# A graph kernel's first layer: TensorE takes the gathered tiles ahead of the count matmuls in each half turn

## The reference, cut to what matters

```python
proj = einsum('nf,hfg->nhg', x, w_proj)
delta = proj[sender] - proj[receiver]
radial_logits = einsum('ehf,hf->eh', delta, radial_score) - scale * edge_len[:, None]
tangential_logits = einsum('ehf,hf->eh', delta, tangential_score)
# per receiver: alpha = softmax of the logits over its edges; sum of alpha * delta
out = seg_softmax_msg(radial_logits) + seg_softmax_msg(tangential_logits)
x = layernorm(x + (x + nan_to_num(out.mean(axis=1)) @ w_out))
```

## Time and profile before

| | |
|---|---|
| median of 3 runs | 3445.18 us (3444.8 to 3448.61) |
| the profiled execution | 3443.76 us, its span 3442.0 us |
| mean granted TensorE clock | 0.725 of full speed |
| busy over the span | PE 2513.1 us, DVE 2112.7, POOL 1797.3, ACT 433.8 |
| the changed stage's first and last gather | start at 134.6 and 1278.3 us |

### The profile page before, as it was taken

The page is one execution under the profiler, slowest core; times in us unless marked ns, Lnnn a source line. Parts: engine busy times, 40 slices in busy tenths (PEclk is TensorE's granted clock), DMA queues, the critical chain, the costliest instruction groups (busy, mean ns, idle before and its releaser), DMA issues. The chain is left out here.

```text
span 3442.0 us, 63721 instructions
## 1 busy us (share of the span) xinstructions
PE 2513.1 (73%) x13080; PEld 1967.7 (57%) x13081; DVE 2112.7 (61%) x7932; ACT 433.8 (13%) x1043; POOL 1797.3 (52%) x1867
## 2 busy tenths in 40 slices
PE   1477777777777776896647634888888899888836
PEld 1244454444444443554637633888888888888826
DVE  5477777777777764543332332777777777777743
ACT  0011111111111111111000001111111111111100
POOL 0377777777777760000010011777777777777710
PEclk6699989999999997997857855555555555555558
DMA  1344444444444451000000001333333333333410
GB/s 36 95 119 120 122 119 119 122 122 117 121 122 119 120 111 26 16 12 1 7 0 1 1 1 34 80 82 81 81 81 82 81 82 82 82 81 82 79 18 10
DMA packets 415827, 246.81 MB, mean 72 GB/s; under 512 B 327579, under 2 KB 372618, under 8 KB 415754
## 3 DMA queue, kind: packets, MB, share of 16 engines
q0 software_dynamic: 71040, 176.52, 20.2%
q1 hardware_dynamic: 281786, 47.96, 7.4%
q10 hardware_dynamic: 62928, 21.43, 2.4%
HBM read 231.37 MB, written 14.34 MB: 71 GB/s over the span
## 5 line engine op out<-in xcount | busy, mean ns | idle before, releaser
L860 POOL DMA_INDIRECT edges_rows<-table,edges_idx x888 | 874.4, 985 | 273.0 <-issue 213.9
L1672 POOL DMA_INDIRECT edges_rows<-table_kv,edges_idx x888 | 855.6, 964 | 276.7 <-issue 257.6
L983 PE MATMUL edges_radial_ps<-edges_rows,edges_into_w 128*128 x1776 | 480.4, 408 | 237.4 <-SPq L870 212.9
L983 PEld LDWEIGHTS edges_radial_ps<-edges_rows,edges_into_w 128*128 128x128 f32 x1776 | 322.2, 194 | 390.1 <-issue 352.2
L1863 PE MATMUL edges_acc<-edges_values,edges_into 128*128 128x136 f32 x1776 | 511.4, 461 | 41.8 <-DVE edges_values L1752 31.3
L1863 PEld LDWEIGHTS edges_acc<-edges_values,edges_into 128*128 128x128 f32 x1776 | 416.6, 328 | 81.0 <-DVE edges_values L1752 66.3
L915 DVE TENSOR_SCALAR edges_cell<-edges_ramp,edges_strip_key,first_key 128x400 bf16<-128x400 f16 x1184 | 452.7, 382 | 0.0
L1840 PE MATMUL edges_q_ps<-attention_q,edges_into_t 128*128 (+1 forms) x1782 | 441.8, 421 | 0.0
L1840 PEld LDWEIGHTS edges_q_ps<-attention_q,edges_into_t 128*128 128x128 f32 x1782 | 416.3, 334 | 0.0
L1717 DVE TENSOR_SCALAR edges_ahead<-edges_nodes,edges_starts,edges_dst_f 128x128 bf16<-128x128 f32 x894 | 261.2, 358 | 174.7 <-issue 174.7
L914 DVE TENSOR_SCALAR edges_low<-edges_places,first_src_low 128x128 bf16<-128x128 bf16 x1184 | 329.2, 278 | 0.1
(11 more groups left out here) (343 smaller groups left out, 2241.4 us busy)
## 6 DMA issues: line engine op xcount, KB each, us to landing
edges_values<-in_edge_attr SPq DMA_DIRECT2D x888, 32.0 KB
edges_rows<-table,edges_idx POOLq DMA_INDIRECT x888
edges_rows<-table_kv,edges_idx POOLq DMA_INDIRECT x888
edges_attr<-in_edge_attr ACTq DMA_DIRECT2D x51, 256.0 KB
edges_bias<-bias_kept SPq DMA_DIRECT2D x296, 12.0 KB
bias_kept<-edges_bias_out ACTq DMA_DIRECT2D x52, 64.0 KB
table<-all_counts SPq DMA_DIRECT2D x1, 3250.0 KB, 11.4
radial<-edges_radial_out ACTq DMA_DIRECT2D x25, 130.0 KB
```

Source lines behind the costliest of these rows:

```text
L860: pool.indirect_dma_start(rows[:, n, :], None, table0, bass.IndirectOffsetOnAxis(ap=idx[:, n:n + 1], axis=0)).then_inc(s_rows[g], 16)
L983: last = nc.tensor.matmul(radial_ps[:, 0:ROW0], into_w[:, h, j, :], rows[:, bass.ds(slot + h * G + j, 1), :].squeeze(1), start=False, stop ...
L1672: pool.indirect_dma_start(rows[:, n, :], None, table_kv, bass.IndirectOffsetOnAxis(ap=idx[:, n:n + 1], axis=0)).then_inc(s_rows[g], 16)
```

## The change

In each half turn PE now waits for the landed rows and for `into_w` first and does the three matmuls of gathered rows; then it waits for the one-hots of the counts and does the four count matmuls, and the last of these raises `s_half`. No instruction is added or removed, and the loops of the other engines stand as they were.

```diff
                                     for h in range(2):
-                                        pe.wait_ge(s_fro, 2 * v + h + 1)
-                                        for q in range(Q):
-                                            nc.tensor.matmul(cells_ps[:, q, 0:KEY], low[:, h, q, :], cell[:, h, q, :], start=False, stop=True,
-                                                             skip_group_check=True)
                                         pe.wait_ge(s_landed, 2 * v + h + 5)
                                         pe.wait_ge(s_into, 2 * v + h + 2)
                                         for j in range(G):
-                                            last = nc.tensor.matmul(radial_ps[:, 0:ROW0], into_w[:, h, j, :],
-                                                                    rows[:, bass.ds(slot + h * G + j, 1), :].squeeze(1),
-                                                                    start=False, stop=True, skip_group_check=True)
+                                            nc.tensor.matmul(radial_ps[:, 0:ROW0], into_w[:, h, j, :],
+                                                             rows[:, bass.ds(slot + h * G + j, 1), :].squeeze(1),
+                                                             start=False, stop=True, skip_group_check=True)
+                                        pe.wait_ge(s_fro, 2 * v + h + 1)
+                                        for q in range(Q):
+                                            last = nc.tensor.matmul(cells_ps[:, q, 0:KEY], low[:, h, q, :], cell[:, h, q, :], start=False, stop=True,
+                                                                    skip_group_check=True)
                                         last.then_inc(s_half, 1)
```

## The result

The changed kernel ran at 3517.94 us (median of 4, 3517.39 to 3518.94) against 3446.0 us for the kernel before in the same comparison: a ratio of 1.0208, 95% interval 1.019 to 1.0226. The forecast was 3448 us, its range ended at 3462 us. It was wrong.

The account below looks back on a forecast made before the run. The prediction took POOL's gathers to bound the stage. It summed 0 (steady) + 2 (low clock) + 0.7 (end) + 0 (gathers) to about +3 us on 3443.76, giving 3446.8, and 3448 us as median; range 3435 to 3462 us.

Parts of the forecast that it names:

- What bounds the kernel: Changed stage: POOL's gathers bound it at 23.3 us a side; DVE at 22.25 us has 1.0 us to spare.
- PE's work and the start of the tiles: PE in each half: tiles start unchanged, priced at nothing; `s_half` comes 2.26 us after it instead of 1.58.
- the low clock: Short low-clock stretches of the stage: counts before `s_half` take 1.1 us more per half; priced at 2 us, at most 12.
- the clock rival: Side starts: PE stands still some 1 us longer, clock falls more often; five sides at 4.7 us, 3470 us; chance 0.13.
- the delay doesn't pile up from side to side: DVE's index copies: fourth half's tiles hang on the rows' landing, so POOL resets DVE each side; steady sides cost nothing.
- The cover: Next side's index copy ahead of its gather: 2.7 us, 2.1 us at a window's start, against a copy 0.46 us late.
- DVE's loop as the bound at full clock: Rival: PE's tile-to-count switch costs 0.15 us more, so DVE's side reaches 23.3 us; 3450 to 3460 us; chance 0.10.
- POOL's wait for row buffers: POOL waits for the half four before, ended over two halves of 3.88 us earlier; 0.68 us delay covered: nothing.
- the end of the stage: After the last tiles, count matmuls now precede ACT's cast: +0.68 us, once; other side ends 0.
- The gathers: POOL's gathers slowed beside DVE: 34 us of excess dealt anew, bounds 17 us less or more, middle nothing.
- What would have shown it: Wrong if POOL pauses before line 860 exceed 5 us in sum, clock under 0.9, or mean gather over 8 ns from 985.
- signs of being right: POOL's gathers back to back in about 1144 us, DVE's short waits for PE well over a hundred, PE's landed-row wait grown.

Follow-up runs that it names:

- e12: Kernel before with one more DVE instruction in each half, a comparison into a spare tile that nobody reads: 3479.2 us, profiled execution 3469.27 us.
- e7: Changed kernel with one of the three `into_w` of each half left out on DVE, so the radial sums are not the reference's: 3435.47 us.
- e1: Changed kernel with 18 added matmuls of zeros on PE at each side's start, behind the clears: 3444.96 us.
- e10: Kernel before with 5 matmuls of zeros between tiles and `s_half`, plus 18 at each side's start: eleven runs from 3439.68 to 3445.43 us.
- e9: Kernel before with 18 matmuls of zeros on PE at each side's start: ratio 0.9994.
- e2: Kernel before, counts still first, with 5 matmuls of zeros between the gathered tiles and `s_half`: ten runs from 3436.11 to 3492.17 us.
- e6: Changed kernel with 9 added matmuls of zeros on PE at each side's start: ten runs from 3446.65 to 3481.10 us.
- e5: Kernel before with one added wait: in each turn's first half PE waits for `into_w` before the counts, which still stand first: 3478.35 us.
- e8: Changed kernel's PE order, with DVE making the three `into_w` before the eight one-hots of the counts: 3451.99 us.
- e11: Kernel before with tiles first only in each turn's second half, plus 18 matmuls of zeros at each side's start: 3450.84 us.
- e4: Kernel before with tiles first only in each turn's second half: nine of ten runs at 3438.9 to 3447.1 us, one at 3456.2.

## Why the prediction was wrong

**What bounds the kernel: right.** POOL bound the stage before, DVE was second, and e12 and e7 show both sides of its margin. The margin was read a little too large: 22.25 us is the side without line 893, and every second side has some 0.65 us more on DVE, so that the mean slack against 23.3 us is an estimated 0.7 us and not 1.0.

**PE's work and the start of the tiles: half right.** Tiles and counts together take 2.25 us at full clock (645.34 to 647.59 in the changed kernel's timeline), forecast 2.26. But "the start is unchanged" held only where rows came last, and in the changed kernel they did so four times (4.8 us of waits for them).

**The step that failed is the low clock.** The forecast took the clock of before as given, 50 us of low stretches, looked at what the new order costs inside them, and priced that at 2 us in its sum, at most 12. Measured, POOL's new pauses are 95.0 us, of which shorter gathers gave 22.9 back. The change made new low stretches: in the changed kernel there is one at 48 of 50 side starts, and the clock over the stage is 0.90 for 0.98. The clock was not a setting under which the change runs, it was one of its results. The delay of one `s_half` was well worked out in the clock rival: 3.7 to 4.2 us behind the tiles, measured 3.95 and 4.30. The rival counted five sides at 4.7 us; it was nearly all 50, at 1.4 us each (72.1 / 50), since the low stretch covers a side's first half and at most part of the next, and DVE waits for PE once in a side and not in each of its three pairs. So the rival's 3470 us has the right mechanism with both factors off, one too low and one too high.

**Why all sides and not five: the loop.** The rival lengthened PE's stand-still by about 1 us, to some 2 us. At the stage's second side it was just that, and the clock fell behind it; at the third it had doubled (PE's rows of the changed kernel):

```profile
167.12 2.80 PE L979 MATMUL edges_radial_ps<-edges_rows,edges_into_w 128*128 x6 [2.07 <-DVE edges_into_w L920]
...
192.03 2.96 PE L979 MATMUL edges_radial_ps<-edges_rows,edges_into_w 128*128 x6 [4.08 <-DVE edges_into_w L920]
```

It stays at 3.5 to 4.2 us in all later sides but the last, because DVE is late by then and PE waits at a side's start for DVE alone. The last tiles of a side show the turn, in the kernel before and in the changed one:

```profile
624.56 1.58 PE L983 MATMUL edges_radial_ps<-edges_rows,edges_into_w 128*128 x6 [1.61 <-SPq L870]
```

```profile
653.58 1.58 PE L979 MATMUL edges_radial_ps<-edges_rows,edges_into_w 128*128 x6 [0.26 <-DVE edges_into_w L920]
```

Before, the rows landed last, PE ended its side late and its next wait for DVE was short. Now PE ends right behind DVE, and DVE's side end of 8.5 to 9.2 us, less PE's own work in it, is stand-still. The argument "the delay doesn't pile up from side to side: POOL itself sets DVE's place again" is true as long as the fourth half's tiles hang on the landing; in the changed kernel they hang on `into_w` (242 waits), and nothing sets DVE back. The kernel before has the beginning of the same loop in its trace: the clock is low around the starts of four sides in a row, from 441.05 to 512.36 us (part of it in the 0.93 of the earlier trace rows), the step from the second to the third index copy is 3.3 to 4.2 us in place of 2.7, PE's stand-still rises to 1.99 us, and then it dies out before POOL has to wait.

**The cover was read too large.** From the index copy's end to the gather that waits for it there are 0.81 us even when POOL stands ready (635.23 to 636.04). The covers of 2.7 and 2.1 us were 1.9 and 1.3 us, and the "1.29 us" of rows 7 was 0.5 us. The kernel before was closer to POOL's first wait than the prediction said.

**DVE's loop as the bound at full clock** (the second rival): refuted by e1. **POOL's wait for row buffers, the end of the stage:** nothing to see, as forecast. **The gathers:** they did move, 22.9 us less in place of nothing, outside the bounds given. In part that follows from the rest, for a POOL that waits has more gathers beside an idle DVE; e10 has 854.6 us with little waiting, so how DVE's and POOL's instructions fall against each other may count as well; that was not isolated.

**What would have shown it** was named rightly: pauses of POOL put down to line 911, of more than 5 us in sum. The other two signs came true as well: the mean gather is 959 ns for 985, and the clock is 0.89 over the whole stage (0.90 from 160 to 1275 us), just under the 0.9 that was named. None of the signs of being right did: DVE waits for PE 49 times and not over a hundred, and PE's wait for landed rows fell.

Of the kernels that do all of the work, none beats the one before by more than can be measured: e10 and e9 lie at 0.9995 and 0.9994 with intervals that reach over 1. Five runs of e2 (3436.1 to 3441.3 us) lie under the median before, 3443.9 us, but the same program also runs at 3492.

What stays open: what exactly decides at a given side whether the clock falls (e6, e12 and the kernel before have sides of both kinds), why e5 loses only 32 us, and why the gathers take 14 us more than their median in one order and 37 in another, with the same instructions on DVE (e10's 854.6 and e8's 878.4 us against 888 x 0.947 = 841).

## What to carry to other kernels

Small PE work that seems to be in the way of the critical tiles may be what keeps PE's clock up through a wait: before moving it, look at how long PE will stand still, at every place where the loop pauses. Where two engines wait for each other through double buffers, add up each one's whole period, pauses of loop ends included, and compare with the bound; if the margin is a few per cent, a local delay of half a microsecond can lock the loop in a slower rhythm, and several runs of one program will then differ by more than any noise. Matmuls of zeros in the pause are a cheap test of whether the clock is the cause, if the trace is asked as well whether the clock rose: in e9 it did not.

## What the runs showed of the hardware

A stand-still of PE costs after it is over: in the side shown the granted clock was 1.00 in 3.20 us in which PE did nothing and 0.58 in the 4.10 us of work behind it. The Trainium skill ("TensorE: Matmul & The Clock Gate", HAM oscillation — how this bites in real kernels) tells of a kernel whose bursts of matmuls each start at the low clock again after waits for DMA; the trace shows the same with waits for VectorE, 48 low stretches in 50 sides. Eighteen matmuls of zeros (2.16 us) hold the clock at 1.00 in e1 and e10; in e9 and e11 it is 0.98 and 0.99, with no low start. Nine leave it at 0.97 in e6, with 16 low starts.

What a low clock costs hangs on where it falls: e4 ran at 0.96 without loss and without a low start, while e6 at 0.97, with 16 of them, lost 17 us in the median, and e12 at 0.94, with 29, lost 25 us in the profiled execution.

Gathers of the same size took 851.5 to 878.4 us for 888 of them in programs whose POOL code is the same: 3% of their time. What DVE does beside them is the suspect; no run isolates it.
